# Four of a token's eight expert rows summed by TensorE through diagonals of scores, and the residual rows read during the expert stage

## The reference, cut to what matters

```python
x = x + _L0_ffn_ref(_layernorm(x), gate_w, w_gate, w_up, w_down)
# in it: 64 experts, each token goes to its 8 best
scores, idx = jax.lax.top_k(probs, TOP_K)
y = jnp.einsum('ecf,edf->ecd', jax.nn.silu(g) * u, w_down)
y_pair = y[e_sorted, safe_pos] * (s_sorted * valid)[:, None]
out = jnp.zeros((N, D)).at[tok_sorted].add(y_pair)
```

## Time and profile before

| what | us |
|---|---|
| median of 3 runs (2484.97 to 2494.7) | 2489.81 |
| the profiled execution | 2486.63 |
| its span | 2484.9 |
| VectorE busy, TensorE busy, whole span | 1786.6, 2136.3 |

### The profile page before, as it was taken

One profiled execution on the slowest core, in us unless ns is written; L12 is line 12 of the kernel. 1 busy time (PEld: TensorE's weight loads), 2 busy tenths in 40 slices (PEclk: granted clock), 3 DMA queues, 4 the chain that ended last, 5 costly groups with the idle time before them and its releaser, 6 DMA issues. The chain is left out here.

```text
span 2484.9 us, 55791 instructions
## 1 busy us (share of the span) xinstructions
PE 2136.3 (86%) x21320; PEld 1461.4 (59%) x21320; DVE 1786.6 (72%) x3776; ACT 1432.3 (58%) x2948; POOL 674.2 (27%) x708
## 2 busy tenths in 40 slices
PE   5999999999999999999999999999995089899940
PEld 3666666566666666666666666666663067666730
DVE  4557777878777778787777878787777655555538
ACT  1667666767676667676666667676765144444410
POOL 1002030312222130303030303121220447766650
PEclk9999999999999999999999999999996589999975
DMA  6486662313132323132232333231310156555647
GB/s 202 165 285 231 201 237 76 82 66 83 68 84 76 73 80 85 66 92 89 60 97 52 97 84 79 70 82 67 84 53 34 43 178 187 174 177 181 185 144 270
DMA packets 132950, 294.14 MB, mean 118 GB/s; under 512 B 22139, under 2 KB 89383, under 8 KB 126544
## 3 DMA queue, kind: packets, MB, share of 16 engines
q1 hardware_dynamic: 114256, 255.89, 33.6%
q0 software_dynamic: 18432, 34.69, 3.9%
HBM read 165.40 MB, written 108.27 MB: 110 GB/s over the span
## 5 line engine op out<-in xcount | busy, mean ns | idle before, releaser
L623 PE MATMUL W<-sb_ident,sb_probs 128*128 128x128 f32 (+1 forms) x3328 | 487.6, 282 | 59.8 <-issue 19.5
L783 ACT ACTIVATE sb_probs<-S,sb_negmax 128x1604 f32<-128x1604 f32 x256 | 409.5, 1600 | 224.0 <-DVE sb_negmax L948 221.7
L775 ACT ACTIVATE sb_probsT<-W 128x384 f32<-128x384 f32 (+1 forms) x1024 | 476.1, 514 | 72.1 <-PE W L623 66.9
L623 PEld LDWEIGHTS W<-sb_ident,sb_probs 128*128 128x128 f32 (+1 forms) x3328 | 366.9, 140 | 189.5 <-issue 93.8
L948 DVE TENSOR_REDUCE sb_negmax<-S 128x1 f32<-128x1604 f32 x256 | 465.9, 1820 | 1.5 <-PE S L613 0.3
L596 PE MATMUL W<-sb_wkv_in,sb_ctx 128*128 128x256 f32 (+1 forms) x1664 | 434.0, 405 | 26.7 <-DVE sb_K_lo L932 13.9
L586 PE MATMUL W<-sb_ctx,sb_wkv_in 128*32 128x401 f32 x4096 | 410.6, 503 | 2.5 <-DVE sb_V L942 2.5
L596 PEld LDWEIGHTS W<-sb_wkv_in,sb_ctx 128*128 128x128 f32 (+1 forms) x1664 | 306.7, 194 | 99.3 <-ACT sb_probsT L775 33.0
L767 ACT ACTIVATE sb_K_hi<-W,sb_pair_cols 128x401 fp32r<-128x401 f32 x256 | 153.0, 598 | 336.8 <-PE W L586 259.0
L932 DVE SCALAR_TENSOR_TENSOR sb_K_lo<-W,sb_pair_cols,sb_K_hi 128x401 fp32r<-128x401 f32 x256 | 161.9, 633 | 223.4 <-ACT sb_K_hi L767 221.5
L1279 POOL DMA_INDIRECT y_scratch<-sb_ys,sb_places x256 | 258.3, 1009 | 112.3 <-issue 91.6
(11 more groups left out here) (181 smaller groups left out, 2819.7 us busy)
## 6 DMA issues: line engine op xcount, KB each, us to landing
sb_ctx<-ctxT SPq DMA_DIRECT2D x32, 1604.0 KB, 7.7
xe_scratch<-sb_none SPq DMA_DIRECT2D x32, 1088.0 KB, 12.5
sb_xg<-xe_scratch SPq DMA_DIRECT2D x64, 544.0 KB
sb_BC<-bc_scratch SPq DMA_DIRECT2D x32, 1024.0 KB, 6.3
sb_Q_hi<-sb_q_hi SPq DMA_DIRECT2D x128, 128.0 KB, 4.4
sb_Q_lo<-sb_q_lo SPq DMA_DIRECT2D x128, 128.0 KB, 5.8
y_scratch<-sb_none SPq DMA_DIRECT2D x16, 1024.0 KB
sb_rows<-y_scratch SPq DMA_DIRECT2D x16, 1024.0 KB, 7.5
```

Of the source, the lines that this page charges most:

```text
L623: ins = pe.transpose(W[0:keys_in(t), at * P:(at + 1) * P], probs[n % 2][:, t * P:t * P + keys_in(t)], ident[:])
L775: act.activation(probsT[k][n % (k + 1)][:, 0:wide], ring[bank_of("T", G, k)][:, 0:wide], ACT.Copy)\
L783: act.activation(probs[n % 2][:].rearrange("p (c k) -> p c k", c=QUADS), scores_of, ACT.Exp, bias=negmax[:, slot:slot + 1], accum_out=den[ ...
```

## The change: what it does

In the combine phase each pair's eight rows are divided. Rows 0 to 3 stay with VectorE's multiply-adds. For rows 4 to 7 ScalarE makes four 128x128 tiles, an identity times the token's score in each partition, and TensorE multiplies each of them by the row tile and sums the four in a PSUM tile `summed`. VectorE adds that tile last. There are two sets of diagonals and two PSUM tiles. GpSimd builds a new identity at the start of the phase. The sum is no longer made in four buffers of its own but in the tile `x3_sb` (128x16x256), which holds all residual rows: one transfer of 2 MB loads it, put into SyncE's order in the expert phase at expert 32, ahead of the down weights. The residual loads of the combine phase and their waits are gone.

```diff
+        X3_AT = E // 2
...
+                if e == X3_AT:
+                    sp.dma_start(dram["x3_sb"][:], dram["x3"].rearrange("(i p) d -> p i d", p=P)).then_inc(dram["x3_in"], 16)
                 after(sp, y_done, e - 1)
                 sp.dma_start(wd[n][:], io["wdT"][bass.ds(e, 1)].rearrange("o f d -> (o f) d")).then_inc(wd_in[n], 16)
...
-        acc = [sb(f"acc{n}", [P, D]) for n in range(DEEP)]
+        ON_PE = 4
+        HERE = TOPK - ON_PE
+        STEPS_HERE = HERE + 1
+        ident = sb("ident3", [P, P])
+        acc = dram["x3_sb"]
         rows = [sb(f"rows{n}", [P, TOPK, D]) for n in range(DEEP)]
+        diag = [sb(f"diag{n}", [P, ON_PE, P]) for n in range(2)]
+        summed = [ctx.enter_context(nc.psum_tensor(f"summed{n}", [P, D], F32)) for n in range(2)]
...
+        @block.gpsimd
+        def _(pool):
+            pool.memset(ident[:], 0.0).then_inc(ident_up, 1)
+            pool.wait_ge(ident_up, 1)
+            pool.affine_select(out=ident[:], in_=ident[:], compare_op=ALU.not_equal, fill=1.0, base=0,
+                               pattern=[[-1, P]], channel_multiplier=1).then_inc(ident_up, 1)
+
+        @block.scalar
+        def _(act):
+            act.wait_ge(ident_up, 2)
+            for i in range(PAIRS):
+                if i >= 2:
+                    act.wait_ge(sum_up, i - 1)
+                for k in range(ON_PE):
+                    ins = act.activation(diag[i % 2][:, k, :], ident[:], ACT.Copy, scale=score(i, HERE + k))
+                ins.then_inc(diag_up, 1)
+
+        @block.tensor
+        def _(pe):
+            for i in range(PAIRS):
+                n, turn = i % DEEP, i // DEEP + 1
+                pe.wait_ge(diag_up, i + 1)
+                if i >= 2:
+                    pe.wait_ge(acc_up, STEPS_HERE * (i - 1))
+                pe.wait_ge(y_in[n], 16 * turn)
+                for k in range(ON_PE):
+                    ins = pe.matmul(summed[i % 2][:], diag[i % 2][:, k, :], rows[n][:, HERE + k, :],
+                                    start=(k == 0), stop=(k == ON_PE - 1))
+                ins.then_inc(sum_up, 1)
...
             def load(i):
-                n, before = i % DEEP, i // DEEP
-                after(sp, acc_up, TOPK * (i - DEEP + 1))
+                n = i % DEEP
+                after(sp, acc_up, STEPS_HERE * (i - DEEP + 1))
                 sp.dma_start(rows[n][:], ...)
-                after(sp, o_out[n], 16 * before)
-                sp.dma_start(acc[n][:], dram["x3"][i * P:(i + 1) * P, :]).then_inc(x_in[n], 16)
...
+            dve.wait_ge(dram["x3_in"], 16)
             for i in range(PAIRS):
                 n, turn = i % DEEP, i // DEEP + 1
-                dve.wait_ge(x_in[n], 16 * turn)
                 dve.wait_ge(y_in[n], 16 * turn)
-                for t in range(TOPK):
-                    dve.scalar_tensor_tensor(acc[n][:], rows[n][:, t, :], scores[:, i * TOPK + t:i * TOPK + t + 1], acc[n][:],
+                for t in range(HERE):
+                    dve.scalar_tensor_tensor(acc[:, i, :], rows[n][:, t, :], score(i, t), acc[:, i, :],
                                              ALU.mult, ALU.add).then_inc(acc_up, 1)
-                    dve.wait_ge(acc_up, i * TOPK + t + 1)
+                    dve.wait_ge(acc_up, i * STEPS_HERE + t + 1)
+                dve.wait_ge(sum_up, i + 1)
+                dve.tensor_tensor(acc[:, i, :], summed[i % 2][:], acc[:, i, :], ALU.add).then_inc(acc_up, 1)
```

More of the change, by code:

```diff
@@ L1422, in combine_phase, with score @@
         DEEP = 4
-        acc = [sb(f"acc{n}", [P, D]) for n in range(DEEP)]
+        ON_PE = 4
[3 more added lines that the diff above has]
+        acc = dram["x3_sb"]
         rows = [sb(f"rows{n}", [P, TOPK, D]) for n in range(DEEP)]
+        diag = [sb(f"diag{n}", [P, ON_PE, P]) for n in range(2)]
+        summed = [ctx.enter_context(nc.psum_tensor(f"summed{n}", [P, D], F32)) for n in range(2)]
         scores = dram["scores_sb"]
-        x_in = [sem(f"cx_in{n}") for n in range(DEEP)]
         y_in = [sem(f"cy_in{n}") for n in range(DEEP)]
         o_out = [sem(f"o_out{n}") for n in range(DEEP)]
+        ident_up = sem("ident_up")
+        diag_up = sem("diag_up")
+        sum_up = sem("sum_up")
         acc_up = sem("acc_up")
         block = ctx.enter_context(nc.Block())
+        def score(i, t):
+            return scores[:, i * TOPK + t:i * TOPK + t + 1]
+        @block.gpsimd
[25 more added lines that the diff above has]
+                ins.then_inc(sum_up, 1)
         @block.sync
@@ L1445, in _ @@
                     load(i + DEEP - 1)
-                sp.wait_ge(acc_up, TOPK * (i + 1))
-                sp.dma_start(out[i * P:(i + 1) * P, :], acc[i % DEEP][:]).then_inc(o_out[i % DEEP], 16)
+                sp.wait_ge(acc_up, STEPS_HERE * (i + 1))
+                sp.dma_start(out[i * P:(i + 1) * P, :], acc[:, i, :]).then_inc(o_out[i % DEEP], 16)
             for n in range(DEEP):
@@ L1472, in perceiver @@
         mixer_phase(nc, ins, dram)
+        dram["x3_sb"] = ctx.enter_context(nc.sbuf_tensor("x3_all", [P, PAIRS, D], F32))
+        dram["x3_in"] = ctx.enter_context(nc.semaphore("x3_in"))
         expert_phase(nc, ins, dram)
```

## The result

| | before | after |
|---|---|---|
| median of 5 runs, us | 2486.24 (2484.93 to 2494.7) | 2472.12 (2465.72 to 2473.37) |
| the profiled execution, its span | 2486.63, 2484.9 | 2472.12, 2470.4 |
| first row load of the last stage to the end of the span | 74.0 | 53.5 |
| start of the span to that load | 2410.86 | 2416.90 |

The ratio of the two kernels' runs is 0.9922, 95% interval 0.99 to 0.9944; the two medians of the table differ by less, 14.1 us or 0.9943, which is that interval's upper end. 2470 was predicted. Two more comparisons, in other groups of runs, gave 0.9908 (0.9892 to 0.9923) and 0.9920 (0.9904 to 0.9937). The last stage lost 20.5 us, as forecast.

A forecast was written before the change was run, and what follows sets the result against it. VectorE's multiply-adds bound the last stage, then transfers at 2.97 us a pair. Span 2484.9 - 20.5 + 1.0 = 2465.4; with 1.7 for the execution 2467.1, the median 3.2 above it: 2470 predicted, range 2461 to 2480.

The forecast's parts named there:

- The bound and its cover: Last stage: VectorE's multiply-adds bind at 4.16 us a pair and thinly cover transfers, whose DMA engines are 86% busy.
- The rival in which VectorE stays the bound: Last stage: stores slip in free and VectorE's 2.53 us a pair binds; end 2458.7, time 2465; chance 0.12.
- The serial loop: Last stage: diagonals, products and release run serially, 5.2 us a pair, 83.4 in all, time 2508; chance 0.04.
- The signs of being wrong: VectorE's waits ending mostly on TensorE, landed rate well under 390 GB/s, or the stage starting more than 1 us later.
- The third sign: Last stage: a landed transfer rate well under 390 GB/s would show the forecast wrong.
- The stream: Last stage's row loads and stores: from 2413.0, 40.7 us of rows and 5.6 of thirteen stores, last landing 2459.3.
- the price of a small transfer: Last stage: each 128 KB store or residual load takes 0.43 us, from 13.9 us shared by 32.
- the cold start: TensorE runs pairs 0 and 1 at low clock, putting VectorE 2.4 us behind, made up later where transfers set the pace.
- The rival of a clock that stays at half: Last stage: TensorE's clock stays at half or falls repeatedly, 3.5 us a pair, time 2480; chance 0.17, partial form included.
- its partial form: Last stage: TensorE's clock is at half for half the time, time 2474; chance 0.10.
- The residual load: Expert stage: the moved 2.10 MB load is mostly absorbed, costing 1 us; rival, its whole 6.9 us, time 2476, chance 0.08.
- The sum: Whole kernel: span 2484.9 less 20.5 plus 1.0 is 2465.4; execution 2467.1; predicted time 2470.

The follow-up runs named there:

- the move alone: Kernel before with only the residual load moved to the expert phase, VectorE doing all eight rows: stage 73.8 us, ratio 0.9995.
- two rows on TensorE: Changed kernel with two rows of each pair on TensorE and six on VectorE: stage 62.5 us, ratio 0.9929 to the kernel before.
- half of the rows loaded: Changed kernel loading only the first four rows, which TensorE multiplies in place of rows 4 to 7 (output wrong): stage 47.5 us, ratio 0.9887.
- the clock held up: Changed kernel plus idle TensorE products from the last expert to the first rows and two behind each pair's sum: stage 51.9 us, ratio 0.9917.
- six rows on TensorE: Changed kernel with six rows of each pair on TensorE and two on VectorE: stage 53.7 us, ratio 0.9916 to the kernel before.
- after on that chip: Changed kernel unaltered, run a third time on the chip of the run with the clock held up: stage 53.6 us, ratio 0.9920 to the kernel before.
- a load over eight: Changed kernel making the 2 MB residual load at eight experts instead of one: experts 396.2 us, stage 56.6 us, ratio 0.9927 to the kernel before.

## Why the prediction was right

**The bound and its cover.** That VectorE held the old stage alone, and that transfers would take over, is shown by the move alone (nothing), two rows on TensorE (62.5, VectorE's sum), half of the rows loaded (6.0 us less) and the clock held up (VectorE waits for rows alone). The rival in which VectorE stays the bound is out, though not by much: sixteen pairs of 2.42 us are 38.7 of the 46.4 us that it takes from its first to its last instruction. The serial loop is out too: six rows on TensorE cost nothing, and the stage isn't near its 83 us.

**The signs of being wrong.** Of the three that the prediction names, one came and one came in part. The stage started 6.0 us later, not within 1; the paragraph on the residual load takes that up. And while VectorE's waits as a whole end mostly on rows, those behind the first data don't: 4.7 us for TensorE against 1.9 for rows (21.1 less the first, 19.2).

```profile
DVE x_all L1501 <- DMA sb_rows<-y_scratch: 21.1, 6, 19.2
DVE x_all L1505 <- PE summed L1473: 4.7, 4, 1.8
```

The transfers ran on through these waits (the share stays at 1.01), so the stream of rows and stores still set the stage's length; but VectorE's waits alone would have pointed at TensorE. The third sign, a rate well under 390 GB/s, didn't come.

**VectorE, ScalarE.** The durations were right (485 and 425 ns); a pair back to back takes 2.42 us (2428.49 to 2430.91 in after's timeline), not 2.53, as the addition overlaps its neighbour. ScalarE's four took 1.28 us from first to last rather than 1.56, since one starts before the other ends.

**The transfers.** The stream was forecast to last 46.3 us (2413.0 to 2459.3) and lasted about 46.5 (some 2419.0, 2.1 us after the first issue as before, to 2465.55). Two errors cancel in this, and that the stage came out at 53.5 to a tenth is luck. The first is the price of a small transfer: I took 0.43 us, and it is 0.3. The residual load of a pair costs 0.31 (3.13 - 2.82), and a store 2.82 - 2.54 = 0.28. Thirteen of them are 3.7 us, not 5.6. The step that failed is the one that got 13.9 us for 32 transfers out of the share. It had an error of reading: 72.9% is of the 80 us of the window that was asked for, not of the 74.9 in it, which is 58.3 us, and the windows agree (0.79 x 74). But the corrected figure would have been further off, 0.55. The share is no price list: it grows when the queue isn't kept full. In a window from 2390 to 2480 the hardware queue shows 58.5% for the move alone and 52.6% for after, that is 52.7 and 47.3 us for the same 18.88 MB:

```profile
q1 hardware_dynamic: 4608, 18.88, 58.5%
```

That is the queue's row (packets, MB, share of 16 engines) for the move alone; the same row for after:

```profile
q1 hardware_dynamic: 4608, 18.88, 52.6%
```

**TensorE's clock.** The other error: I let the cold start be made up later at no cost and counted no falls. Holding the clock up gained 1.7 us. So 40.7 + 3.7 + 1.7 makes 46.1, near the 46.5 measured. Cold for the first pairs and then mostly at full clock was as forecast (0.50, then 0.93, 0.76 and 0.93 in the windows of after). The rival of a clock that stays at half is out for this kernel; its partial form is what happened, at 1.7 us rather than the 4 that 2474 stands for. How a slower TensorE lowers the rate of the transfers, at a share that stays near 1, is not shown. Argued only: pairs that end late free their blocks late, so that loads and stores go out in bunches. It fits that the fifth row load went out 9.3 us after the first in after on that chip (2359.30) and 7.8 us with the clock held up (2357.83).

**The residual load.** I took 1 us, between 0 and 6.9. Measured are 0.3 us a load over eight, and 1.7 between one load and none, which one execution each can't tell from nothing: the move alone, which has the load, took 393.8 against 393.7 without it. TensorE did stop, as forecast: it was busy for 15.76 of the 18 us from 2191, the load's issue among them, where before it was busy for all 18, and the stop was mostly hidden. The load's engine time was over-priced with the same 0.43: that stretch has a DMA share of 0.88, where such a stretch had 0.61, so some 4.9 us, and sixteen times 0.31 is 5.0. The 6.0 us by which the profiled execution of after came late to its last stage are not the load's: 2.6 were there at the first expert, in a phase that the change doesn't touch, and 4.2 ahead of the load; over the load it was 5.3 and, an expert later, 4.4. The 3.4 us by which the expert stage was longer, more than the one or two that were forecast, are of the same kind.

**The sum.** Forecast were 19.5 us off the time before; the ratio of 0.9922 stands for 19.4 of 2486, its interval for 14 to 25, and the medians differ by 14.1. The 2470 was reckoned from 2489.81 for the kernel before, which the five runs put at 2486.24, and 2472.12 was measured; that the two figures agree within 2.1 us is in part luck, as single executions of either kernel differ by 8 to 10.

## What to carry to other kernels

When one engine's chain is the bound and transfers lie under it, the gain of shortening the chain is read from the bytes over the rate of a full queue (here 412 GB/s, from the stretch in which several loads were waiting), not from the DMA share, which was 0.86 where a full queue would have done the same work in less. Taking transfers out of a stage is worth nothing until they bind, and then 0.3 us for 128 KB. TensorE, newly given a little work in each step, started cold and fell back; holding the clock up gained 1.7 us here, where it had a third of its time to spare, and one execution with three falls was 2.5 to 3 us longer than the others, for a cause that stays open.

## What the runs showed of the hardware

- In the run with the clock held up, row loads of 8 KB pieces came at 415 to 430 GB/s with 1 KB stores between them, over 44 us. The Trainium skill (DMA: Bandwidth & Descriptors, Where 436 GB/s comes from) names about 358 GB/s of HBM as what binds such transfers; the trace doesn't agree, and is nearer to the 435 that it gives for the fabric.
- TensorE's clock fell amid work: in after TensorE waited 1.90 us before 2433.40 and ran at 0.60 in the next window, and again 1.95 us before 2443.14, with 0.57 in the window after that. With waits of 0.8 to 1.0 us in each pair from 2451 on it stayed at 1.00. The two rows are of its timeline.

```profile
2433.40 5.38 PE L1473 MATMUL summed<-sb_rows,sb_diag 128*128 128x256 f32 x16 [1.90 <-DVE x_all L1505]
...
2443.14 7.54 PE L1473 MATMUL summed<-sb_rows,sb_diag 128*128 128x256 f32 x24 [1.95 <-DMA sb_rows<-y_scratch]
```

- The same kernel had spans of 2470.4, 2453.7 and 2403.6 us in three groups of runs, the last two of them on different chips. The last stage was 53.5, 54.2 and 53.6; the difference lies in the stages ahead of it, most of it ahead of the experts' first scatter (2014.2, 2004.2 and 1954.4).
